# Cross-attention and expert layer: the row maxima by half units of four heads

## The reference

```python
q = Wq @ layernorm(x) + bq;  k = Wk @ ctx + bk;  v = Wv @ ctx + bv       # per batch, 256 x 512
dot  = einsum('bhdt,bhds->bhts', q, k) / 4                                # 16 heads, 512 x 512
dot  = mask * dot - (1 - mask) * 1e6
x    = x + (softmax(dot, axis=-1) * mask) @ v
x    = x + experts(layernorm(x))                                          # top 2 of 8, SiLU gate, fp32
```

## Time and profile before

| what | value |
|---|---|
| median of 3 runs | 927.23 us (927.05 to 927.42) |
| profiled execution | 925.97 us, its span 924.2 us |
| ahead of the first score tile | 59.13 us |
| from there to the last product of unit 15 | to 571.46 us |
| routing's tail, to the first matmul of the experts | to 615.90 us |
| experts | to 924.2 us |
| busy: TensorE, VectorE, ScalarE, GpSimd | 815.2, 551.8, 317.0, 371.3 us |

### The profile page before, as it was taken

One profiled execution on the slowest core, in us unless ns is written; L12 is line 12 of the kernel. 1 busy time (PEld: TensorE's weight loads), 2 busy tenths in 40 slices (PEclk: granted clock), 3 DMA queues, 4 the chain that ended last, 5 costly groups with the idle time before them and its releaser, 6 DMA issues. The chain is left out here.

```text
span 924.2 us, 12981 instructions
## 1 busy us (share of the span) xinstructions
PE 815.2 (88%) x3769; PEld 372.9 (40%) x3770; DVE 551.8 (60%) x1044; ACT 317.0 (34%) x615; POOL 371.3 (40%) x392
## 2 busy tenths in 40 slices
PE   4878899999989998999999888129999999999994
PEld 1233333333333332333333322116656666665662
DVE  5856588888878887888778762333333333333331
ACT  0014465555655655555566566000000000000000
POOL 6507255555745665665574242401211222212122
PEclk9559899999999999999999999559999999999998
DMA  7632668665865856765564422342456455453332
GB/s 213 200 82 92 200 196 243 201 206 176 270 181 157 278 185 179 222 181 181 178 200 144 128 76 85 103 148 51 98 128 153 77 146 120 109 156 68 68 68 34
DMA packets 84561, 138.26 MB, mean 150 GB/s; under 512 B 14737, under 2 KB 40657, under 8 KB 84514
## 3 DMA queue, kind: packets, MB, share of 16 engines
q1 hardware_dynamic: 68658, 108.27, 38.6%
q0 software_dynamic: 7744, 17.86, 9.9%
q10 hardware_dynamic: 8112, 11.55, 4.3%
HBM read 77.37 MB, written 59.36 MB: 148 GB/s over the span
## 5 line engine op out<-in xcount | busy, mean ns | idle before, releaser
L812 DVE TENSOR_REDUCE mx<-tile 128x2 f32<-128x1024 f32 x256 | 309.1, 1217 | 77.7 <-PE tile L1121 67.6
L703 ACT ACTIVATE pr<-sc 128x512 f32<-128x512 f32 x512 | 269.2, 601 | 213.1 <-PE sc L1108 210.5
L1121 PE MATMUL tile<-qk 97*128 97x512 bf16 x480 | 147.3, 390 | 27.2 <-DVE mx L812 16.1
L1108 PE MATMUL sc<-qk 100*128 100x512 bf16 x512 | 155.7, 385 | 10.9 <-DMA qk<-mxt 7.5
L1460 POOL DMA_INDIRECT out_dram<-y,ids x36 | 56.1, 1558 | 258.8 <-DVE ids L1381 254.8
L1148 PE MATMUL pvb<-pr,vp 128*32 128x512 f32 x1024 | 138.0, 611 | 0.0
L1440 ACT ACTIVATE sg<-gp 128x352 f32<-128x352 f32 x36 | 16.7, 463 | 266.7 <-PE gp L1481 266.7
L1513 PE MATMUL dp<-wring,at 128*128 (+1 forms) x216 | 98.8, 593 | 1.6 <-DVE at L1391 1.6
L1121 PEld LDWEIGHTS tile<-qk 97*128 97x128 bf16 x480 | 34.1, 98 | 158.4 <-DVE mx L812 74.5
L1481 PE MATMUL gp<-wring,xtile 128*128 x288 | 93.7, 469 | 1.1 <-DVE meta L1372 1.1
L1481 PE MATMUL up<-wring,xtile 128*128 x288 | 91.2, 460 | 0.0
(11 more groups left out here) (126 smaller groups left out, 777.2 us busy)
## 6 DMA issues: line engine op xcount, KB each, us to landing
qk<-stack_d SPq DMA_DIRECT2D x32, 768.0 KB
stack_d<-parts SPq DMA_DIRECT2D x32, 384.0 KB, 2.8
wring<-w_dram SPq DMA_DIRECT2D x32, 352.0 KB, 5.5
xl<-routed_d ACTq DMA_DIRECT2D x38, 257.0 KB, 2.7
stack_d<-parts SPq DMA_DIRECT2D x32, 256.0 KB, 3.0
pv_d<-ov SPq DMA_DIRECT2D x32, 256.0 KB, 4.2
xin<-x_dram SPq DMA_DIRECT2D x16, 256.0 KB, 5.3
cin<-ctxt_dram SPq DMA_DIRECT2D x8, 512.0 KB, 6.1
```

Of the source, the lines that this page charges most:

```text
L703: nc.scalar.activation(pr[s % 2][:, j, :], sc[(32 * u + 4 * s + j) % NSC][:, :], ACT.Exp, scale=SCALE).then_inc(exped.sem, 1)
L812: dve.tensor_reduce(cols, t[:, :, :], X, ALU.max, negate=True).then_inc(drained.sem, 1)
L1108: nc.tensor.matmul(sc[(32 * u + 4 * s + j) % NSC][:, :], ks[half(u)][0:ALL_ROWS, h, c * P:c * P + P], qs[half(u)][0:ALL_ROWS, h, :], start ...
L1121: last = nc.tensor.matmul(t[:, i, :], qs[half(w)][0:RAW_ROWS, h, c * P:c * P + P], ks[half(w)][0:RAW_ROWS, h, :], start=True, stop=True)
```

## The change

The maxima are handled by half units. Each group g of four heads has its own transposition (16 columns), split and DMAs. The raw pairs run eight pairs later: the steps 0 and 1 of unit n hold pairs 12 to 15 of unit n itself, steps 2 to 7 pairs 0 to 11 of unit n+1. Group 1 of unit n is transposed at the end of step 2 of unit n and awaited by the scores of its step 4; group 0 of unit n+1 is transposed at the end of step 6 of unit n and awaited by step 0 of unit n+1. Before the first step there are 12 raw pairs: 8 as `first_raw`, 4 as `raw_scores`. The values of unit 0 move ahead of the transposed maxima, layernorm of units 1 and 2 behind the raw pairs, and that of unit 4, with the k and q projection of unit 2, into unit 0.

```diff
-LEAD = 4
+LAG = 4
 def pairs_of(n, s):
-    first = LEAD + 2 * s
-    if first < NPAIR:
-        return [first, first + 1] if has(n + 1) else []
-    return [first - NPAIR, first - NPAIR + 1] if has(n + 2) else []
+    first = 2 * s - LAG
+    if first < 0:
+        return [first + NPAIR, first + NPAIR + 1] if has(n) else []
+    return [first, first + 1] if has(n + 1) else []
 def fillers(n, s):
-            + (["maxT"] if s == 6 and has(n + 1) else [])
+            + ([("maxT", 1)] if s == 2 and has(n) else []) + ([("maxT", 0)] if s == 6 and has(n + 1) else [])
...
         def heads_in(eng, heads):                 # SyncE: range(2), ScalarE: range(2, 4); before 4 and 4
...
-            def keep_maxima(u):
+            def keep_maxima(u, g):
+                w = u + 1 - g
+                sp.wait_ge(maxsplit.sem, maxsplit.at(u, (g, 2)))
+                if (due := scored.at(w - 2, (4 * g + 3, 3))) is not None:
                     sp.wait_ge(scored.sem, due)
                 for i in range(3):
+                    sp.dma_start(qs[half(w)][MAX_ROW + i:MAX_ROW + i + 1, 4 * g:4 * g + 4, :]
...
                 if has(u - 2):
                     store_x1(u)
+                if u and has(u):
+                    keep_maxima(u, 1)
                 if has(u - 1):
                     store_recip(u)
...                                                 # GpSimd, unit 0
                 if has(u + 2):
                     part(u, 1)
+                if u == 0:
+                    part(-1, 0)
+                    batch_rstd(-1)
...                                                 # VectorE, unit(u), around step 2
+                maximum(u, 0)
+                token_normalize(u, 0)
+                maximum(u, 1)
+                token_normalize(u, 1)
+                split_maxima(u, 1)
                 if u == 0:
                     projection_out(-1, 0)
+                    normalize(-1)
+                maximum(u, 2)
...                                                 # TensorE
                 if s == 0 and j == 0:
-                    pe.wait_ge(maxrows.sem, maxrows.at(u - 1, "m"))
+                    pe.wait_ge(maxrows.sem, maxrows.at(u - 1, 0))
+                if s == 4 and j == 0:
+                    pe.wait_ge(maxrows.sem, maxrows.at(u, 1))
...
                 if m % 8 == 0:
-                    pe.wait_ge(stacked[m // 8].sem, stacked[m // 8].at(u, "g"))
+                    pe.wait_ge(stacked[m // 8].sem, stacked[m // 8].at(w - 2 + m // 8, "g"))
...
+            for m in range(8):
                 first_raw(-1, m)
             pe.wait_ge(const_loaded, CONST)
+            values(-1)
...
+            transpose_maxima(-1, 0)
+            for m in range(8, NPAIR - LAG):
+                raw_scores(-1, m)
```

More of the change, by code:

```diff
@@ L108, in fillers @@
             + (["xT"] if s == 4 and has(n - 2) else []) + (["logits"] if s == 5 and has(n - 2) else [])
-            + (["maxT"] if s == 6 and has(n + 1) else []) + (["k"] if s == 7 and has(n + 3) else []))
+            + ([("maxT", 1)] if s == 2 and has(n) else []) + ([("maxT", 0)] if s == 6 and has(n + 1) else []) + (["k"] if s == 7 and has(n + 3) else []))
 def tile_events(n):
@@ L300, in attention @@
         vmade = Count(sem("vmade"), of(1, "v"))
-        maxsplit = Count(sem("maxsplit"), of(1, "p0", "p1", "p2"))
-        maxrows = Count(sem("maxrows"), of(1, "m"), 48)
+        maxsplit = Count(sem("maxsplit"), lambda n: [(g, i) for g in (1, 0) if has(n + 1 - g) for i in range(3)])
+        maxrows = Count(sem("maxrows"), lambda n: [g for g in (1, 0) if has(n + 1 - g)], 48)
         den_in = Count(sem("den_in"), of(-1, "d"), 16)
@@ L500, in _ @@
             sp.wait_ge(mf_kept, 16)
[L501 to L504, removed]
+            sp.dma_start(qf[D::GROUP, :, :], mf_d.rearrange("(o s) t -> o s t", o=1).broadcast_to([4, 2, T])
+                         ).then_inc(qf_in, 16)
+            heads_in(sp, range(2))
             sp.wait_ge(mask_made, 4)
@@ L650, in _ @@
             values_out(-1)
-            batch_rstd(-1)
-            part(-1, 0)
+            batch_rstd(-3)
+            batch_rstd(-2)
             for u in range(LAST + 1):
@@ L803, in maximum @@
                     return
-                if j == 0 and (due := ready.at(u - 1, "maxT")) is not None:
+                if j == 0 and (due := ready.at(u - 1, ("maxT", 1))) is not None:
                     dve.wait_ge(ready.sem, due)
@@ L1053, in _ @@
             projection_out(-2, 1)
-            for j in range(LEAD):
-                maximum(-2, j)
+            for j in range(4):
+                maximum(-1, j)
+            dve.wait_ge(const_loaded, CONST)
+            dve.tensor_copy(upper[:, :], utf[:, :]).then_inc(const_made, 1)
+            dve.wait_ge(const_made, MADE)
+            for j in range(4, 8):
+                maximum(-1, j)
+            values_out(-1)
+            split_maxima(-1, 0)
+            for j in range(8, NPAIR - LAG):
+                maximum(-1, j)
             for u in (-3, -2):
@@ L1127, in first_raw @@
                 t = slot(u, ("max", m))
-                g, c, j = m // 8, m % 8 // 2, 2 - 2 * (m % 2)
+                c, j = m // 2, 2 - 2 * (m % 2)
                 for i in range(2):
                     at = GROUP * (j + i)
-                    both = qf[at:at + D + 1, g, :, :]
-                    last = nc.tensor.matmul(t[:, i, :], both[:, 0, c * P:c * P + P], both[:, 1, :],
-                                            start=True, stop=True)
+                    last = nc.tensor.matmul(t[:, i, :], qf[at:at + D + 1, 0, c * P:c * P + P],
+                                            qf[at:at + D + 1, 1, :], start=True, stop=True)
                 last.then_inc(ready.sem, 1)
@@ L1212, in ranks, with transpose_maxima @@
                                  ).then_inc(ready.sem, 1)
-            def transpose_maxima(u):
-                if not has(u + 1):
+            def transpose_maxima(u, g):
+                w = u + 1 - g
+                if not has(w):
                     return
-                pe.wait_ge(drained.sem, drained.at(u, ("max", NPAIR - 1)))
-                t = slot(u, "maxT")
-                nc.tensor.transpose(t[0:32, 0, 0:P], mx[:, half(u + 1), :], idf[:, :]).then_inc(ready.sem, 1)
+                pe.wait_ge(drained.sem, drained.at(u, ("max", 8 * g + 7)))
+                t = slot(u, ("maxT", g))
+                nc.tensor.transpose(t[0:16, 0, 0:P], mx[:, half(w), 16 * g:16 * g + 16], idf[:, :]
+                                    ).then_inc(ready.sem, 1)
             def unit(u):
@@ L1262, in _ @@
             project(-2, 1)
[L1263 to L1266, removed]
+            pe.wait_ge(qf_in, 5 * 16)
+            for m in range(8):
                 first_raw(-1, m)
             pe.wait_ge(const_loaded, CONST)
+            values(-1)
             pe.wait_ge(const_made, MADE)
             pe.wait_ge(ones_made, 4)
[L1271 to L1276, removed]
+            transpose_maxima(-1, 0)
+            for m in range(8, NPAIR - LAG):
+                raw_scores(-1, m)
             for u in range(LAST + 1):
```

128 lines of the change are left out of this document (53 added, 75 removed).

## The result

The changed kernel took 980.49 us, median of 4 runs (976.66 to 985.76); the kernel before, on the same chip, 927.33 us (927.05 to 928.64). The ratio is 1.0573, its 95% interval 1.0539 to 1.0606: slower, by some 53 us. The profiled execution, the fastest of the four, has a span of 974.9 us, against 924.2. The prediction was 942 us, with a range of 927 to 953.

What follows compares the result with a forecast made beforehand. Attention was taken as a chain of TensorE, VectorE and back. Terms -14.5 + 15.1 + 10.6 - 1.5 + 5 = +14.7 us on 925.97 gave 940.7, with the median 1.26 higher 942 us, range 927 to 953.

Steps and rivals of the forecast that it cites:

- Item 1, the fill: Ahead of the loop: fewer raw pairs first, first score tile at 41.7 us instead of 59.13, gain 17.4 us.
- Item 2, unit 0: Unit 0: VectorE waits for GpSimd's root, 63.8 to 70.3; net gain with the fill 14.5 us, between 10 and 20.
- the upper bound of 20: Fill and unit 0: net gain if VectorE has no wait for the root in unit 0, 20 us.
- Item 3, the second tile: Steps 3 and 4: another maxima tile in the ring, 1.3 us for units 2 to 12, 0.8 in unit 1, sum 15.1.
- Item 3, the landing: Step 4: maxima issued from 213.0 land 1.83 + 1.29 us later, at 216.1, the score tile at 216.2.
- The upper bound of 2.5 us a unit: Inner units: cost if the maxima's DMA lands late behind the product's loads, issued just ahead by SyncE, 2.5 us each.
- Rival (b): Inner units: new DMA late as a rule, 1 us in 12 units plus 4 for the clock; 953 us, chance 0.16.
- Item 4, units 13 to 15: Last units: no q projection covers the landing in 13 and 14; with unit 15 and lower clock, sum 10.6 us.
- Item 5: Small terms: waits for stacked operands go, 1.5 us; late landings of the new maxima cost 5 us.
- (a): Whole kernel: fill wins, slack swallows the split, units cost under 0.5 us more; 917 us, chance 0.12.
- (c): Whole kernel: gain and loss cancel, fill gain 20 and no late landings; about 927 us, chance 0.10.

Runs made afterwards that it cites:

- e1: The changed kernel with GpSimd making the root for unit 4's layernorm ahead of the split of unit 2's q: 967.47 us, ratio 1.0438.
- e2: The changed kernel with SyncE issuing the second group's maxima ahead of the three 256 KB transfers (product, x, x1): 957.69 us, ratio 1.0323.
- e3: The changed kernel with the second group's maxima issued on ScalarE's queue, behind its step 3 exponentials: 975.48 us, ratio 1.0552.
- e7: The changed kernel with product and x loads cut to 16 rows of 128 from the second unit on: 962.52 us, ratio 1.0368.
- e4: The kernel before plus a second tile of maxima transposed and split into a spare buffer, no DMA or wait: 940.83 us, ratio 1.0143.
- e8: e4 plus three 4 KB DMAs to a spare buffer, issued where the changed kernel does and awaited at step 4: 996.25 us, ratio 1.0727.
- e10: The kernel before with only the second token_normalize of a unit moved from step 2 to step 4: 921.2 us, ratio 0.9943.
- e5: The changed kernel with the edits of e1 and e2 together: 953.65 us, ratio 1.0284.

## Why the prediction was wrong

- **Item 1, the fill:** right. 40.94 us for 41.7. (Its terms put the end of the split at 38.6, not 38.4.) The same fill took 43.0 to 43.4 us in e1, e2, e3 and e7, so that it is right within 2 us, and 0.8 is luck.
- **Item 2, unit 0:** right, in mechanism and size: VectorE's stand 6.62 for 6.5, TensorE's 7.01 for about 6.2, net gain 15.2 for 14.5. e1 shows the root as its cause: without that wait unit 1 begins 19.4 us early (89.90 for 109.29), where the upper bound of 20 ("no such wait") had it, although its maxima are 1.49 us late.
- **Item 3, the second tile:** right for what the ring and VectorE cost in a unit: 3.89 us in step 3, and 1.3 in steps 3 and 4 together in e4. That e4's +14.9 us meets the sum of 15.1 is in part luck, as said there.
- **Item 3, the landing: the step that failed.** "the maxima themselves, issued from 213.0, are there 1.83 + 1.29 later ... at 216.1". The 1.29 us came from the maxima of step 6, which have no loads just ahead. Those of step 2 follow 768 KB, and in the units that waited they land 1.7 us (unit 8) to 5.8 us (unit 3) behind the last issue. The mean step 4 of units 2 to 12 is 2.58 us longer than before, not 0.24. The upper bound of 2.5 us a unit in all, which named this mechanism, was too low as well: tile and landing came to 3.6 a unit.
- **Rival (b)** was this mechanism, priced at 1 us in 12 units and 4 us for the clock. Its "the new DMA is late as a rule" holds (19 waits), its price doesn't: units 2 to 12 alone give 23 us over the forecast. Its place, "behind four issues in SyncE's queue", is half of it: e2 shows that being behind the loads counts, e3 that another queue doesn't help, e7 that their bytes count.
- **Item 4, units 13 to 15:** direction right, size wrong, 22.2 us for 10.6. The wait for a landing at P + 7.6 rested on the same 1.29 us; units 13 and 14 have step 4 at 7.64 and 7.10, and step 5 at 5.19 and 4.49 for the lower clock.
- **Item 5:** the stacked operands' waits went, as said (the products of steps 2 and 0 come 0.09 and 0.07 us sooner, in the mean of units 2 to 12). The 5 us for late landings should have been some 26 (11 times the 2.58 of step 4, less the 0.24 that item 3 has).
- **The sum of misses:** 36.0 us (50.7 - 14.7): 23.0 in units 2 to 12, 11.6 behind them, 1.7 in unit 1, 0.4 in tail and experts, less 0.7 in front. In the inner units the long step is step 4, by the landing, and step 5 behind it, by the clock. That e8 has a loss of this size in the old order (69.1 us, its step 4 as long as here) makes it shown and not only argued; for unit 1 and the end alone no run was made.
- **Rivals (a) and (c)** fell on the same step: (a) wanted an inner unit to cost under 0.5 us more, and it costs 3.7; (c) wanted no late landings, and there are 19 waits.

Open: why landing differs so from unit to unit. In unit 3 the first 256 KB load is issued 1.7 us ahead of the maxima (173.25 and 174.93), in unit 11 it is 4.0 us (460.94 and 464.95), and the landing takes 5.8 and 2.2 us; in unit 5 it is 2.4 and 3.6. That fits; units 2 (1.7 and 2.4) and 10 (4.5 and 2.9) fit less well, and e7 cut two of the three transfers and only a third of the wait. GpSimd's indirect stores of the routed rows run in the same stretch, and no run moved them. Nor did a run take away the read of the next stacked operands, 768 KB, which SyncE issues 1.1 us behind the last maxima of unit 3 (178.07), well before they land. In unit 14, with the loads 7.6 us ahead and no such read behind, the landing is still 2.05 us, not 1.29. The lateness at step 0 in e2 isn't settled either.

## What to carry to other kernels

Take the landing of a small DMA from a row that has the same transfers in flight, not from the same DMA in a quieter place; where no such row exists, the time of all the bytes ahead of it is not an upper bound. Here 768 KB at the 319 to 334 GB/s of unit 3's gap would be some 2.4 us, an estimate, and the landing took up to 5.8. A gain in the fill comes once, a tile more in the ring comes with every unit: 0.9 us in each of 11 inner units, with the ends, ate all of 20 us. And look first for work on VectorE just ahead of a drain that TensorE waits for: moving 0.54 us of it won 5.5 us in e10, 3.3 of them in the step it was aimed at, where the whole change, mended, won nothing.

## What the runs showed of the hardware

- A 4 KB DMA took about as long from issue to landing as one of 8 KB: medians of 1.7 us (group 0 in e3) and 1.8 us (e8) in the same quiet place. With the loads in flight 4 KB took 2.7 us on ScalarE's queue and 3.1 on SyncE's. The Trainium skill, "DMA: Bandwidth & Descriptors", section "Anatomy of one DMA — SWDGE (gpsimd) path", says of GpSimd's path that the fixed cost doesn't scale with the size; on SyncE's queue the traces show the same for these two sizes.
- Long waits cost twice. The clock fell to the lower of its two levels (1.2 GHz) behind waits of 5.23, 4.45, 3.36 and 2.15 us (records of 1.03 or 1.04 us instead of 0.60, at 182.78, 142.26, 537.20 and 327.98), and the next step then took up to 5.19 us instead of 3.89. Behind one of 2.51 us (257.91) it didn't fall, and behind one of 1.64 us (203.69) it did, 3 us later (records of 1.03 at 206.97; the step took 4.46 us instead of 2.83), so the length alone doesn't decide. A wait in the changed kernel is thus up to 1.6 us dearer than the profile's list of waits says.
- The times of one kernel spread by about 1% in both kernels: 976.66 to 985.76 us after, and 923.00 to 931.31 in the 13 runs of the kernel before beside e5 to e8. That its four runs beside the result lie within 1.6 us is no measure of its spread, and differences of 2 or 3 us between kernels of four runs were not told apart here. The fill varies too: with the same code ahead of them the values of unit 0 started at 31.27 and 34.43 us in two executions (after and e1).
